# Edge MLP of a graph network: the second layer's bias copied into the message's PSUM bank by ScalarE, in place of a product with rows of ones

## The chip, the cores and the metric

The kernel runs on one core of a Trainium2 chip. The metric is the device time of one execution in microseconds. A core has TensorE (matmuls, results into PSUM, a memory of eight banks of 128 partitions x 512 float32), VectorE and ScalarE (elementwise work, both read and write SBUF and PSUM), GpSimd (here it issues gathers and scatters) and SyncE (issues plain DMAs). Each engine works through its own instructions in order, and semaphores order them between engines.

## The reference

Four graph layers run over the same 625 nodes of 512 features and 10625 edges. Each gets the normed, rectified rows `h` of `x`, and its result is added to `x`. The change lies in the third one, whose edge part is:

```
src, dst = (edge_index[0], edge_index[1])
edge_feat = jnp.concatenate([x[src], x[dst], edge_attr], axis=-1)
h = mish(edge_feat @ W1 + b1)
messages = mish(h @ W2 + b2)
agg = jax.ops.segment_sum(messages, dst, num_segments=x.shape[0])
```

with `mish(x) = x * tanh(softplus(x))`, 64 edge attributes, and `b2` a row of 512 values drawn with a spread of 0.1. The node part behind it and the fourth layer are untouched.

## The kernel before, in words

The products of the node features with W1 are made ahead for all nodes and stored as two tables in HBM. The edges are sorted by destination group into NS = 87 blocks of 128 edges. The stage of interest walks over these blocks; between this stage and its neighbours stands a barrier of all engines.

**Per block t**, in the order of the data:

- GpSimd gathers the row of table i for each edge and adds that of table j by a second gather (`gather_i` L1007, `add_j` L1015), nine blocks in flight.
- TensorE, `pre(t)` (L1156): four transposes of that sum into one bank (L1164), then four products of the edge attributes with their part of W1 on top (L1167, eight passes), so that the bank holds the hidden layer before its mish, turned.
- mish is worked out from e = exp(z) as z * (1 - 2 / (e * (e + 2) + 2)). ScalarE makes the exponential out of the bank (`grow_exp(0, t)`, L1119). VectorE clamps it (L1063) and makes e * (e + 2) (`top`, L1065). ScalarE takes the logarithm (`log_of`, L1124) and the exponential of its negative (`invert`, L1129), which is the reciprocal. VectorE multiplies with the bank (`finish_hidden`, L1072, semaphore mish0); the factor -2 sits in W2, scaled once at L1100.
- TensorE: the bias product (`bias(t)`, L1175), 64 rows of ones by 64 rows of which three hold b2 split into three bf16 parts and the others zero, into the same bank, which it starts anew. Then `message(t)` (L1184), eight passes of hidden x W2 on top of it.
- The same chain of ScalarE and VectorE with layer index 1 gives the message (`finish_message`, L1087, semaphore mish1). ScalarE rounds it (`high_part`, L1135), VectorE takes the remainder (`split_message`, L1094, semaphore mes_lo).
- VectorE makes a 128x128 table of which edge goes to which node (`one_hot`, L1080); TensorE adds both parts of the message over the edges by two products with it (`seg_sum`, L1199) into one of five banks.

Banks 5, 6 and 7 turn round; `pre(t)` and `message(t)` use the same one for every t of 1 and more, so that `pre(t + 3)` waits for mish1 of block t.

**The order** is written by hand, one turn s after the other, on each engine:

```
TensorE:  message(s-1); pre(s+1), with bias(s) inside it; seg_sum(s-2)
ScalarE:  exp of message s-1; exp of hidden s+1; log and invert of message s-1;
          log and invert of hidden s+1; high_part(s-1)
VectorE:  clamp and top of message s-1; one_hot(s-1); clamp and top of hidden s+1;
          finish_message(s-1); finish_hidden(s+1); split_message(s-1)
```

`bias(s)` stands behind the first attribute product of `pre(s+1)` and waits for mish0 of block s. The last block's bias stands ahead of its own message.

**Ahead of the first turn** TensorE turns the attributes of all blocks (88 transposes, L1208), ScalarE copies them out (L1139), VectorE makes the ones, the zeros and the three parts of b2 (L1048 to L1057), and SyncE loads b2 (2 KB, L986), the attribute weights (L987) and W2 (L988), and puts the three parts of b2 into place with three DMAs (L992).

Of the kernel before, what the change touches and what calls it, by code (L numbers as in the profile page):

```python
# [8 lines left out]
F32 = mybir.dt.float32  # L9
F32R = mybir.dt.float32r  # L10
BF16 = mybir.dt.bfloat16
FP16 = mybir.dt.float16
I32 = mybir.dt.int32
ALU = mybir.AluOpType
# [3 lines left out]
P = 128  # L18
N = 625
E = 10625  # L20
D = 512
# [23 lines left out]
def gnn_stack(nc, a, out):  # L45
    ctx = ExitStack()
    with ctx:
        def sb(name, shape, dt, where=ctx):
            return where.enter_context(nc.sbuf_tensor(name, shape, dt))
# [909 lines left out]
        with p3:  # L959
# [1 line left out]
            attr = sb("attr", [ED, SC * P], F32, p3)  # L961
            w_attr = sb("w_attr", [ED, D], F32, p3)
            w2 = sb("w2", [P, KT, D], F32, p3)
            b2_in = sb("b2_in", [1, D], F32, p3)
            b2_rows = sb("b2_rows", [P, D], BF16, p3)[ED:P, :]
            ones = sb("ones", [P, P], BF16, p3)[ED:P, :]
            pair_sum = sb("pair_sum", [P, GOT3, D], F32, p3)
            grow = [sb(f"grow{l}", [P, 2, D], F32, p3) for l in range(2)]
            hidT = sb("hidT", [P, 2, D], F32, p3)
# [2 lines left out]
            mes_lo = sb("mes_lo", [P, 2, D], F32R, p3)  # L972
            is_dst3 = sb("is_dst3", [P, HOT3, P], F32R, p3)
            none = mes[:, 0, :].bitcast(BF16)[:, 0:D]
            b2_flat = mes[0:1, :, :].rearrange("p b o -> p (b o)").bitcast(BF16)
            b2_part = [b2_flat[:, (j + 1) * D:(j + 2) * D] for j in range(3)]
            idx = rec[:, :, 0:2].bitcast(I32)
            pre_bank = lambda t: 5 + max(2 * t - 1, 0) % 3
            mes_bank = lambda t: 5 + (2 * t + 2) % 3
            N_TURN = SC // TURN_GROUP  # L980

# [1 line left out]

            @block.sync
            def _(sp):
                sp.dma_start(b2_in[:], a["b2_row"]).then_inc(sem("b2_in"), 16)  # L986
                sp.dma_start(w_attr[:], a["L2_gnn_W1"][2 * D:2 * D + ED, :]).then_inc(sem("w_attr_in"), 16)  # L987
                sp.dma_start(w2[:], a["L2_gnn_W2"].rearrange("(k p) o -> p k o", p=P)).then_inc(sem("w2_in"), 16)  # L988
                sp.wait_ge(sem("b2_split"), 6)
                sp.wait_ge(sem("b2_zero"), 1)  # L990
                for j in range(3):
                    sp.dma_start(b2_rows[j:j + 1, :], b2_part[j]).then_inc(sem("b2_rows"), 16)  # L992
                sp.wait_ge(sem("mes_mm"), 2)
                sp.dma_start(w3[:], a["L2_gnn_W3"].rearrange("(k p) o -> p k o", p=P)).then_inc(sem("w3_in"), 16)
                sp.dma_start(w4[:], a["L2_gnn_W4"].rearrange("(k p) o -> p k o", p=P)).then_inc(sem("w4_in"), 16)
                sp.dma_start(rows_in2[:], a["in_rows_in2"].broadcast_to((P, 4 * D)).rearrange("p (r o) -> p r o", r=4)).then_inc(sem("rows2_in"), 16)
                sp.dma_start(b3_col[:], a["in_b3_col"]).then_inc(sem("b3_in"), 16)
# [47 lines left out]
            @block.vector  # L1045
            def _(dve):

                nc.vector.memset(b2_rows, 0.0).then_inc(sem("b2_zero"), 1)  # L1048
                nc.vector.memset(ones, 1.0).then_inc(sem("b2_ones"), 1)
                nc.vector.memset(none, 0.0).then_inc(sem("none"), 1)  # L1050
                dve.wait_ge(sem("b2_in"), 16)
                for j in range(3):
                    if j:
                        dve.wait_ge(sem("b2_split"), 2 * j)
                    nc.vector.tensor_copy(b2_part[j], b2_in[:]).then_inc(sem("b2_split"), 1)
                    dve.wait_ge(sem("b2_split"), 2 * j + 1)
                    nc.vector.tensor_tensor(b2_in[:], b2_in[:], b2_part[j], ALU.subtract).then_inc(sem("b2_split"), 1)  # L1057

                def grown(l, t):

                    u = grow[l][:, t % 2, :]
                    dve.wait_ge(sem(f"exp{l}"), t + 1)
                    nc.vector.tensor_scalar(u, u, CLAMP, None, ALU.min).then_inc(sem(f"clamp{l}"), 1)  # L1063
                    dve.wait_ge(sem(f"clamp{l}"), t + 1)
                    nc.vector.scalar_tensor_tensor(u, u, 2.0, u, ALU.add, ALU.mult).then_inc(sem(f"top{l}"), 1)  # L1065

                def finish_hidden(t):

                    dve.wait_ge(sem("inv0"), t + 1)
                    if t >= 2:  # L1070
                        dve.wait_ge(sem("mes_mm"), t - 1)
                    nc.vector.scalar_tensor_tensor(hidT[:, t % 2, :], grow[0][:, t % 2, :], -0.5, PS[:, pre_bank(t), :],  # L1072
                                                   ALU.add, ALU.mult).then_inc(sem("mish0"), 1)

                def one_hot(t):
                    if t == 0:
                        dve.wait_ge(sem("rec_in"), 16)
                    if t >= HOT3:
                        dve.wait_ge(sem("sum_mm3"), t - HOT3 + 1)
                    nc.vector.tensor_scalar(is_dst3[:, t % HOT3, :], slot_of_col[:], rec[:, t, 2:3], None,  # L1080
                                            ALU.is_equal).then_inc(sem("is_dst3"), 1)

                def finish_message(t):
                    dve.wait_ge(sem("inv1"), t + 1)
                    if t >= 2:
                        dve.wait_ge(sem("mes_lo"), t - 1)
                    nc.vector.scalar_tensor_tensor(mes[:, t % 2, :], grow[1][:, t % 2, :], -0.5, PS[:, mes_bank(t), :],  # L1087
                                                   ALU.add, ALU.mult).then_inc(sem("mish1"), 1)

                def split_message(t):  # L1090
                    dve.wait_ge(sem("mes_hi"), t + 1)
                    if t >= 2:
                        dve.wait_ge(sem("sum_mm3"), t - 1)
                    nc.vector.tensor_tensor(mes_lo[:, t % 2, :], mes[:, t % 2, :], mes_hi[:, t % 2, :].bitcast(F32),  # L1094
                                            ALU.subtract).then_inc(sem("mes_lo"), 1)

                for s in range(-1, NS + 1):
                    if s == -1:
                        dve.wait_ge(sem("w2_in"), 16)
                        nc.vector.tensor_scalar(w2[:], w2[:], -2.0, None, ALU.mult).then_inc(sem("w2_scaled"), 1)  # L1100
                    if 0 <= s - 1 < NS:
                        grown(1, s - 1)
                        one_hot(s - 1)
                    if 0 <= s + 1 < NS:
                        grown(0, s + 1)
                    if 0 <= s - 1 < NS:
                        finish_message(s - 1)
                    if 0 <= s + 1 < NS:
                        finish_hidden(s + 1)
                    if 0 <= s - 1 < NS:  # L1110
                        split_message(s - 1)

            @block.scalar
            def _(act):
# [16 lines left out]
                def high_part(t):  # L1131
# [2 lines left out]
                        act.wait_ge(sem("sum_mm3"), t - 1)  # L1134
                    nc.scalar.copy(mes_hi[:, t % 2, :], mes[:, t % 2, :]).then_inc(sem("mes_hi"), 1)  # L1135

                for j in range(N_TURN):
                    act.wait_ge(sem("attr_tp"), j + 1)
                    nc.scalar.copy(attr[:, j * D:(j + 1) * D], PS[0:ED, j % 8, :]).then_inc(sem("attr_T"), 1)  # L1139
                for s in range(-1, NS + 1):  # L1140
                    if 0 <= s - 1 < NS:
                        grow_exp(1, s - 1, mes_bank(s - 1))
# [7 lines left out]
                        invert(0, s + 1)  # L1150
                    if 0 <= s - 1 < NS:
                        high_part(s - 1)

            @block.tensor
            def _(pe):
                def pre(t):  # L1156

                    pe.wait_ge(sem(f"pair3_{t % GOT3}"), 16 * (t // GOT3) + 16)
                    if t == 2:
                        pe.wait_ge(sem("mish0"), 1)  # L1160
                    if t >= 3:
                        pe.wait_ge(sem("mish1"), t - 2)
                    for k in range(KT):
# [2 lines left out]
                    for k in range(KT):  # L1166
                        m = nc.tensor.matmul(PS[:, pre_bank(t), k * P:(k + 1) * P], w_attr[:, k * P:(k + 1) * P],  # L1167
                                             attr[:, t * P:(t + 1) * P], start=False, stop=True, skip_group_check=True)
                        if k == 0 and t:
                            bias(t - 1)  # L1170
                    m.then_inc(sem("pre_mm"), 1)

                def bias(t):
                    pe.wait_ge(sem("mish0"), t + 1)
                    nc.tensor.matmul(PS[:, mes_bank(t), :], ones, b2_rows, start=True, stop=False, skip_group_check=True)  # L1175

                def message(t):

                    chunk = None
                    if t == NS - 1:  # L1180
                        bias(t)
                    o = PS[:, mes_bank(t), :]
                    for k in range(KT):
                        m = nc.tensor.matmul(o, hidT[:, t % 2, k * P:(k + 1) * P], w2[:, k, :], start=False,  # L1184
# [29 lines left out]
                    nc.tensor.matmul(PS[:, c, :], none[:, 0:P], none, start=True, stop=False, skip_group_check=True)  # L1214
                pe.wait_ge(sem("w_attr_in"), 16)
                for s in range(-1, NS + 2):
                    if s == 0:
                        pe.wait_ge(sem("b2_ones"), 1)
                        pe.wait_ge(sem("b2_rows"), 48)
                    if s == 1:  # L1220
                        pe.wait_ge(sem("w2_scaled"), 1)
                    if 0 <= s - 1 < NS:
# [437 lines left out]
```

## Time and profile before

| | |
|---|---|
| median of three runs | 1295.84 us (1293.26 to 1300.98) |
| profiled execution, its own time | 1297.59 us |
| its span | 1295.8 us |
| granted TensorE clock, mean of the span | 0.973 |
| stage of the edge MLP in the trace | 535 to 1052 us |
| steady part of it | about 563 to 1040 us |
| steps | 87 |

The span goes from the first to the last instruction of the profiled execution; its own time has what lies around it as well. Times in the rows are microseconds, mean durations ns. A record's duration has the filling and draining of the engine in it, so the start of the next instruction can lie before the end of the one before. The granted clock is given as a share of the full 2.4 GHz.

### The profile page before, as it was taken

How to read it: one execution, taken by the hardware profiler on the slowest of the kernel's cores; microseconds unless marked ns; L12 is line 12 of the kernel's file. 1: busy time of each engine (PE TensorE's matmuls, PEld its weight loads, DVE VectorE, ACT ScalarE, POOL GpSimd, SP SyncE). 2: the span in 40 equal slices, each digit the busy share in tenths (PEclk: the TensorE clock that was granted, in tenths of full speed). 3: DMA queues.
4: the chain of work that ended last, by engine and by line, in shares of the span. 5: the costliest groups of instructions: out<-in, count | busy, mean ns of one | idle time of the engine just before them, and what ended most of it. 6: DMA issues, size and time to landing. Idle time of an engine off the chain costs nothing. (4 is left out here: it accounts for less than half of the span.)

```text
span 1295.8 us, 15266 instructions
## 1 busy us (share of the span) xinstructions
PE 1214.3 (94%) x4908; PEld 646.6 (50%) x4908; DVE 795.6 (61%) x1576; ACT 556.7 (43%) x975; POOL 510.5 (39%) x442
## 2 busy tenths in 40 slices
PE   7898899599999999899999999999999979899995
PEld 3433433244544444555555555555555546445552
DVE  5764564667322323267778777777778756846663
ACT  1021211210110211357777777777777733225552
POOL 1111111253242000277766666666666100047661
PEclk9999899799999999889999999999999989999998
DMA  8699686555400201496544444444444020036662
GB/s 342 230 342 362 236 316 247 180 185 166 175 15 8 95 1 43 117 221 154 109 94 94 95 97 92 96 91 98 92 96 82 1 68 1 17 123 201 185 183 79
DMA packets 59444, 175.86 MB, mean 136 GB/s; under 512 B 12485, under 2 KB 13029, under 8 KB 52584
## 3 DMA queue, kind: packets, MB, share of 16 engines
q0 software_dynamic: 32496, 76.65, 25.0%
q1 hardware_dynamic: 26872, 98.23, 20.9%
q8 instruction: 43, 0.70, 0.2%
q14 instruction: 33, 0.27, 0.1%
HBM read 160.32 MB, written 14.52 MB: 135 GB/s over the span
## 5 line engine op out<-in xcount | busy, mean ns | idle before, releaser
L1184 PE MATMUL PS<-w,hidT 128*128 128x512 f32 x696 | 315.1, 595 | 0.0
L542 POOL DMA_INDIRECT rec_scratch<-rec_src,slot_row x84 | 99.4, 1184 | 287.6 <-DMA rec_scratch<-rec_src,slot_row 234.1
L1184 PEld LDWEIGHTS PS<-w,hidT 128*128 128x128 f32 x696 | 132.3, 191 | 134.0 <-issue 126.7
L1007 POOL DMA_INDIRECT pair_sum<-table_i,counts_rec x87 | 87.4, 1004 | 219.1 <-POOLq L63 130.7
L1015 POOL DMA_INDIRECT pair_sum<-table_j,counts_rec x87 | 147.6, 1697 | 30.7 <-issue 26.2
L1119 ACT ACTIVATE grow<-PS 128x512 f32<-128x512 f32 x174 | 104.0, 598 | 119.1 <-PE PS L1167 83.9
L1280 POOL DMA_INDIRECT u_space<-table_j,rec x87 | 82.3, 946 | 130.8 <-DMA table_j<-agg_rows 94.1
L269 PE MATMUL PS<-is_src,is_dst 128*128 128x512 bf16 x420 | 111.6, 397 | 20.4 <-DVE is_src L575 19.3
L1124 ACT ACTIVATE grow<-grow,two 128x512 f32<-128x512 f32 x174 | 124.8, 717 | 5.0 <-DVE grow L1065 4.9
L1065 DVE SCALAR_TENSOR_TENSOR grow<-grow 128x512 f32<-128x512 f32 x174 | 120.6, 693 | 6.0
L317 PE MATMUL PS<-w_rel,hT 128*128 128x512 f32 x240 | 107.6, 605 | 13.6 <-DMA w_rel<-w_scratch 11.9
L1129 ACT ACTIVATE grow<-grow 128x512 f32<-128x512 f32 x174 | 109.6, 630 | 5.5
L1167 PE MATMUL PS<-attr,w_attr 64*128 64x128 f32 x696 | 101.5, 286 | 0.0
L1024 POOL DMA_INDIRECT rec_scratch<-rec_src,slot_row x84 | 86.4, 1028 | 38.3 <-issue 23.2
L1063 DVE TENSOR_SCALAR grow<-grow 128x512 f32<-128x512 f32 x174 | 74.4, 428 | 40.0 <-ACT grow L1119 31.0
L1072 DVE SCALAR_TENSOR_TENSOR hidT<-grow,PS 128x512 f32<-128x512 f32 x87 | 59.8, 687 | 58.1 <-ACT grow L1129 58.1
L850 ACT COPY stage<-PS 128x512 f32<-128x512 f32 x48 | 28.1, 586 | 154.6 <-PE PS L299 154.6
L1167 PEld LDWEIGHTS PS<-attr,w_attr 64*128 64x128 f32 x696 | 84.5, 188 | 14.5 <-issue 14.5
L1362 DVE TENSOR_TENSOR pair<-PS,u_space 128x512 f32<-128x512 f32 x87 | 60.2, 692 | 47.5 <-issue 39.7
L1540 PE MATMUL PS<-relu,is_src 128*128 128x512 f32 x174 | 88.5, 592 | 0.0
L269 PEld LDWEIGHTS PS<-is_src,is_dst 128*128 128x128 bf16 x420 | 37.6, 101 | 93.9 <-DVE is_src L575 39.4
L1467 ACT ACTIVATE relu<-pair 128x512 f32<-128x512 f32 x87 | 54.9, 631 | 60.3 <-DVE pair L1362 60.3
(216 smaller groups left out, 1795.2 us busy)
## 6 DMA issues: line engine op xcount, KB each, us to landing
ring<-basis_rows SPq DMA_DIRECT2D x48, 1024.0 KB, 7.4
ring<-basis_low SPq DMA_DIRECT2D x30, 512.0 KB, 4.6
w_scratch<-stage SPq DMA_DIRECT2D x96, 32.0 KB
rec_scratch<-ring POOLq DMA_DIRECT2D x2, 1496.0 KB, 14.8
counts_rec<-rec_scratch SPq DMA_DIRECT2D x1, 2992.0 KB, 10.7
rec_scratch<-rec_src,slot_row POOLq DMA_INDIRECT x168, 3.5
root<-L_gnn_root SPq DMA_DIRECT2D x2, 1024.0 KB, 7.8
w_rel<-w_scratch SPq DMA_DIRECT2D x1, 2048.0 KB
```

The source lines that it names most:

```text
L269: nc.tensor.matmul(PS[:, c, :], is_dst[:, t % HOT, c * P:(c + 1) * P], is_src[:, t % HOT, 0:512], start=first, stop=last, skip_group_check ...
L317: m = nc.tensor.matmul(PS[:, bank, :], hT[:, k, c * P:(c + 1) * P], w[:, k, :], start=(k == 0), stop=(k == KT - 1))
L542: nc.gpsimd.indirect_dma_start(out=rec3_dram, out_offset=bass.IndirectOffsetOnAxis(ap=slot_row[:, 1, t:t + 1], axis=0), in_=rec, in_offset ...
L1007: nc.gpsimd.indirect_dma_start(out=pair_sum[:, t % GOT3, :], out_offset=None, in_=tables[0][0], in_offset=bass.IndirectOffsetOnAxis(ap=idx ...
L1015: nc.gpsimd.indirect_dma_start(out=pair_sum[:, t % GOT3, :], out_offset=None, in_=tables[0][1], in_offset=bass.IndirectOffsetOnAxis(ap=idx ...
L1065: nc.vector.scalar_tensor_tensor(u, u, 2.0, u, ALU.add, ALU.mult).then_inc(sem(f"top{l}"), 1)
L1119: nc.scalar.activation(grow[l][:, t % 2, :], PS[:, bank, :], ACT.Exp).then_inc(sem(f"exp{l}"), 1)
L1124: nc.scalar.activation(u, u, ACT.Ln, bias=two[:]).then_inc(sem(f"ln{l}"), 1)
L1129: nc.scalar.activation(u, u, ACT.Exp, scale=-1.0).then_inc(sem(f"inv{l}"), 1)
L1167: m = nc.tensor.matmul(PS[:, pre_bank(t), k * P:(k + 1) * P], w_attr[:, k * P:(k + 1) * P], attr[:, t * P:(t + 1) * P], start=False, stop= ...
L1184: m = nc.tensor.matmul(o, hidT[:, t % 2, k * P:(k + 1) * P], w2[:, k, :], start=False, stop=(k == KT - 1), skip_group_check=True)
L1540: nc.tensor.matmul(PS[:, bass.ds(chunk, 1), :].rearrange("p c o -> p (c o)"), is_src5[:, t % HOT5, :], relu5[:, t % PAIR5, :], start=False ...
```

## The change

ScalarE writes b2, which now lies in SBUF on all 128 partitions, into the message's bank by a plain copy, `bias(t)`, behind the wait for mish0 of block t. It stands at the end of ScalarE's turn, behind `high_part`. `message(t)` on TensorE waits for that copy and adds onto what lies in the bank. The bias product, the ones, the three-part split of b2 and their DMAs go, and so do TensorE's waits for them and the wait of `pre(2)`. b2 is loaded by one broadcast DMA to 128 partitions, still the first on SyncE's queue, and ScalarE waits for it once ahead of its turns. Block 0 now goes through the same bank in `pre` and `message` (7 in place of 5 for `pre(0)`).

```diff
@@ tiles, banks
-            b2_in = sb("b2_in", [1, D], F32, p3)
-            b2_rows = sb("b2_rows", [P, D], BF16, p3)[ED:P, :]
-            ones = sb("ones", [P, P], BF16, p3)[ED:P, :]
+            b2_all = sb("b2_all", [P, D], F32, p3)
...
-            pre_bank = lambda t: 5 + max(2 * t - 1, 0) % 3
+            pre_bank = lambda t: 5 + (2 * t - 1) % 3
@@ sync
-                sp.dma_start(b2_in[:], a["b2_row"]).then_inc(sem("b2_in"), 16)
+                sp.dma_start(b2_all[:], a["b2_row"].broadcast_to((P, D))).then_inc(sem("b2_in"), 16)
...
-                sp.wait_ge(sem("b2_split"), 6)
-                sp.wait_ge(sem("b2_zero"), 1)
-                for j in range(3):
-                    sp.dma_start(b2_rows[j:j + 1, :], b2_part[j]).then_inc(sem("b2_rows"), 16)
@@ vector
-                nc.vector.memset(b2_rows, 0.0).then_inc(sem("b2_zero"), 1)
-                nc.vector.memset(ones, 1.0).then_inc(sem("b2_ones"), 1)
                 nc.vector.memset(none, 0.0).then_inc(sem("none"), 1)
-                dve.wait_ge(sem("b2_in"), 16)
-                for j in range(3):
-                    if j:
-                        dve.wait_ge(sem("b2_split"), 2 * j)
-                    nc.vector.tensor_copy(b2_part[j], b2_in[:]).then_inc(sem("b2_split"), 1)
-                    dve.wait_ge(sem("b2_split"), 2 * j + 1)
-                    nc.vector.tensor_tensor(b2_in[:], b2_in[:], b2_part[j], ALU.subtract).then_inc(sem("b2_split"), 1)
@@ scalar
+                def bias(t):
+                    act.wait_ge(sem("mish0"), t + 1)
+                    nc.scalar.copy(PS[:, mes_bank(t), :], b2_all[:]).then_inc(sem("bias"), 1)
+
                 for j in range(N_TURN):
...
+                act.wait_ge(sem("b2_in"), 16)
                 for s in range(-1, NS + 1):
...
                     if 0 <= s - 1 < NS:
                         high_part(s - 1)
+                    if 0 <= s + 1 < NS:
+                        bias(s + 1)
@@ tensor
                 def pre(t):
...
-                    if t == 2:
-                        pe.wait_ge(sem("mish0"), 1)
...
-                        if k == 0 and t:
-                            bias(t - 1)
...
-                def bias(t):
-                    pe.wait_ge(sem("mish0"), t + 1)
-                    nc.tensor.matmul(PS[:, mes_bank(t), :], ones, b2_rows, start=True, stop=False, skip_group_check=True)
-
                 def message(t):
...
-                    if t == NS - 1:
-                        bias(t)
+                    pe.wait_ge(sem("bias"), t + 1)
...
-                    if s == 0:
-                        pe.wait_ge(sem("b2_ones"), 1)
-                        pe.wait_ge(sem("b2_rows"), 48)
```

## Rows read from the trace of the kernel before

**Rows 1.** The page, busy time of each engine, share of the span, instructions

```profile
PE 1214.3 (94%) x4908; PEld 646.6 (50%) x4908; DVE 795.6 (61%) x1576; ACT 556.7 (43%) x975; POOL 510.5 (39%) x442
```

**Rows 2.** Busy time by stretch: PE, PEld, DVE, ACT, POOL, then PEclk, DMA share, GB/s

```profile
563.00:1040.00 477.00, 476.88 (x1954) 277.79 (x1951) 377.17 (x680) 360.90 (x596) 302.56 (x244) 1.00 0.47 98
```

**Rows 3.** Timeline of PE, one step: start, us, operation, [idle before <-releaser]

```profile
643.19 3.59 PE L1184 MATMUL PS<-w,hidT 128*128 128x512 f32 x8
646.62 0.60 PE L1164 MATMUL PS<-ident,pair_sum 128*128 128x128 f32 x4
...
647.16 0.39 PE L1175 MATMUL PS<-b_rows,ones 64*128 64x512 bf16 x1
647.36 0.94 PE L1167 MATMUL PS<-attr,w_attr 64*128 64x128 f32 x7
648.23 0.50 PE L1199 MATMUL PS<-mes_hi,is_dst 128*128 128x512 f32 x1
...
648.80 3.60 PE L1184 MATMUL PS<-w,hidT 128*128 128x512 f32 x8
```

**Rows 4.** Timeline of ACT in the same step

```profile
641.20 0.60 ACT L1119 ACTIVATE grow<-PS 128x512 f32<-128x512 f32 x1 [0.38 <-PE PS L1184]
642.73 0.60 ACT L1119 ACTIVATE grow<-PS 128x512 f32<-128x512 f32 x1 [0.93 <-PE PS L1167]
643.22 0.71 ACT L1124 ACTIVATE grow<-grow,two 128x512 f32<-128x512 f32 x1
...
644.54 0.72 ACT L1124 ACTIVATE grow<-grow,two 128x512 f32<-128x512 f32 x1
645.30 0.63 ACT L1129 ACTIVATE grow<-grow 128x512 f32<-128x512 f32 x1
645.83 0.60 ACT L1135 CAST mes_hi<-mes 128x512 fp32r<-128x512 f32 x1
```

**Rows 5.** Timeline of DVE in the same step

```profile
641.83 0.43 DVE L1063 TENSOR_SCALAR grow<-grow 128x512 f32<-128x512 f32 x1 [0.19 <-ACT grow L1119]
642.29 0.69 DVE L1065 SCALAR_TENSOR_TENSOR grow<-grow 128x512 f32<-128x512 f32 x1
642.90 0.32 DVE L1080 TENSOR_SCALAR is_dst<-slot_of_col,counts_rec 128x128 fp32r<-128x128 f32 x1
643.36 0.43 DVE L1063 TENSOR_SCALAR grow<-grow 128x512 f32<-128x512 f32 x1
643.82 0.69 DVE L1065 SCALAR_TENSOR_TENSOR grow<-grow 128x512 f32<-128x512 f32 x1
644.63 0.69 DVE L1087 SCALAR_TENSOR_TENSOR mes<-grow,PS 128x512 f32<-128x512 f32 x1
645.96 0.69 DVE L1072 SCALAR_TENSOR_TENSOR hidT<-grow,PS 128x512 f32<-128x512 f32 x1 [0.65 <-ACT grow L1129]
646.56 0.69 DVE L1094 TENSOR_TENSOR mes_lo<-mes,mes_hi 128x512 fp32r<-128x512 f32 x1
```

**Rows 6.** Timeline of ACT, the second message exponential and the last but one

```profile
567.68 0.60 ACT L1135 CAST mes_hi<-mes 128x512 fp32r<-128x512 f32 x1
568.20 0.60 ACT L1119 ACTIVATE grow<-PS 128x512 f32<-128x512 f32 x1
...
1039.91 0.60 ACT L1119 ACTIVATE grow<-PS 128x512 f32<-128x512 f32 x1 [0.39 <-PE PS L1184]
```

**Rows 7.** Timeline of all engines, first steps and last message product

```profile
555.05 0.69 DVE L1072 SCALAR_TENSOR_TENSOR hidT<-grow,PS 128x512 f32<-128x512 f32 x1 [1.45 <-ACT grow L1129]
...
557.37 5.64 PE L1184 MATMUL PS<-w,hidT 128*128 128x512 f32 x8
563.05 0.60 ACT L1119 ACTIVATE grow<-PS 128x512 f32<-128x512 f32 x1 [2.37 <-PE PS L1184]
...
1041.56 3.70 PE L1184 MATMUL PS<-w,hidT 128*128 128x512 f32 x8
```

**Rows 8.** DMA issues (KB each, us to landing), and the timeline's scaling of w2

```profile
table_i<-ring SPq DMA_DIRECT2D x5, 256.0 KB, 2.0
```

```profile
544.94 1.51 DVE L1100 TENSOR_SCALAR w<-w 128x2048 f32<-128x2048 f32 x1 [4.85 <-DMA w<-L_gnn_W]
```

More of the change, by code:

```diff
@@ L974, in gnn_stack @@
             none = mes[:, 0, :].bitcast(BF16)[:, 0:D]
-            b2_flat = mes[0:1, :, :].rearrange("p b o -> p (b o)").bitcast(BF16)
-            b2_part = [b2_flat[:, (j + 1) * D:(j + 2) * D] for j in range(3)]
             idx = rec[:, :, 0:2].bitcast(I32)
-            pre_bank = lambda t: 5 + max(2 * t - 1, 0) % 3
+            pre_bank = lambda t: 5 + (2 * t - 1) % 3
             mes_bank = lambda t: 5 + (2 * t + 2) % 3
```

## The prediction

> **What bounds the kernel now.** I read the page first. TensorE is busy for 94% of the span, the other engines for 61% and less [rows 1]. A share over the whole span mixes stages with different limits, and the change touches only the edge MLP, so the next view is the busy time of that stage alone. From 563 to 1040 us TensorE is busy for 476.9 of 477.0 us at a granted clock of 1.00 (its 2.4 GHz level), VectorE for 79% and ScalarE for 76% [rows 2]. The reader is to see that TensorE has no gap there, and that the two others have room only on average.
>
> The third view is the timeline of one step, engine by engine. On TensorE a message product starts at 643.19 and the next at 648.80, and every piece in between follows the one before without idle time [rows 3]. From the message exponential of 568.20 to that of 1039.91 [rows 6] there are 84 steps: 471.71 / 84 = 5.616 us each. ScalarE waits twice in a step: 0.38 us for the message product, then 0.93 us for the next block's hidden product [rows 4]. VectorE waits 0.19 us and 0.65 us, both times for ScalarE [rows 5]. So TensorE sets the step now, and the other two follow it with some slack. How much slack is the whole question, and it isn't the 24% of idle time that ScalarE shows. The copy comes at one fixed place in ScalarE's order, so it costs whatever the chain through that place leaves free.
>
> **Removed from TensorE.** The bias product starts at 647.16 and the next piece at 647.36 [rows 3], so it holds TensorE for 0.20 us of each step (its record of 0.39 us runs on beside the next). TensorE alone would then need 5.616 - 0.20 = 5.41 us, and 86 steps of this give 17 us. This gain is real only if nothing else needs more than 5.41 us.
>
> **Added to ScalarE.** 87 copies of 128x512, each behind the wait for `finish_hidden` of the same block (semaphore mish0), last in ScalarE's turn. Queued behind it is the exponential of the next message, and VectorE's whole turn begins with that one. Before, that exponential stood behind `high_part`, which doesn't wait for `finish_hidden`. So a ring closes which the old order left open. I add it up from start to start, from the step of ScalarE and VectorE that starts at 641.20 [rows 4, 5]:
>
> - message exponential 641.20 to its clamp 641.83: 0.63
> - clamp to its product `top1` 642.29: 0.46
> - to `one_hot` 642.90: 0.61. No wait here, it is VectorE's own order; the 0.69 us record overlaps the next by 0.08
> - `one_hot` to the hidden clamp: 0.24. The row shows 0.46, but there the clamp still waits for the hidden exponential, which ends at 643.33. In the new order that exponential starts right behind the message's and is ready in time. So the link is the record of 0.32 less the same overlap of 0.08; bounds 0.24 to 0.32
> - hidden clamp 643.36 to its product 643.82: 0.46
> - to the logarithm 644.54: 0.72
> - to the inversion 645.30: 0.76
> - to `finish_hidden` 645.96: 0.66
> - to the bias copy: 0.72, its record of 0.69 and the 0.03 that passes from VectorE to ScalarE at 644.54
> - bias copy to the next message exponential: 0.52, see below
>
> The sum is 5.78 us. The other branches are inside it. The message logarithm and inversion are done before the hidden logarithm can start (3.12 us into the turn by the first six links; the message branch needs 0.63 + 0.46 + 0.72 + 0.76 + 0.53 = 3.10). `high_part` runs beside `finish_hidden`, as now. The split starts 0.60 behind `finish_hidden` and ends 4.54 + 0.60 + 0.69 = 5.83 us into the turn, so the sum over edges that needs it can't begin before 0.05 us into the next, by my estimate at 0.1 to 0.3; TensorE waits there. From then it needs 0.57 (648.23 to 648.80) and 3.60 us until the message is done [rows 3], so by 4.5 us, 1.3 us before ScalarE comes to read it. `pre` is done another 4.84 - 3.60 + 0.1 us later, at 5.8, and ScalarE reads it at 5.78 + 0.50 = 6.28. TensorE is off the ring.
>
> **Price of the copy.** The trace of before has no ScalarE instruction that writes PSUM. The nearest row is `high_part`, also a plain 128x512 copy out of SBUF, with a message exponential right behind it: 567.68 to 568.20, 0.52 us [rows 6]. The low end is 0.49, the shortest from one full-width ScalarE start to the next (642.73 to 643.22 [rows 4]); the high end is 0.60, the whole record of `high_part` with no overlap at all. I take 0.52, because reading is the same and width decides most. The ring then is 5.75 to 5.86 us by this term, and up to 0.08 more by the `one_hot` link.
>
> The Trainium skill (Perfetto Trace Analysis, Optimizing Scalar/DVE Operations) gives ScalarE a fixed cost of about 93 ns per instruction on SBUF but 51 ns on PSUM. No row here shows a ScalarE write to PSUM; if that rule holds for it, the copy would take an estimated 0.48 us, the ring 5.74 us, and the sum below would be 9.4 us in place of 12.9.
>
> **The ends of the stage.** At the start TensorE stands still inside the second `pre` until `finish_hidden` of block 0 (555.05 + 0.69), runs the bias product, finishes `pre`, and starts the first message at 557.37 [rows 7]. With the copy, `pre` is done long before. The copy runs from 555.77 to 556.4 and the message starts then: -0.9 us. The first step, from 563.05 (5.68 us after 557.37) to 568.20, takes only 5.15 us now, since there is no sum over edges in it; in the ring it takes 5.78: +0.6 us. At the end the last message product starts at 1041.56 [rows 7], 1.65 us after the message exponential of 1039.91 [rows 6]; without the bias product and with the split done earlier relative to ScalarE it starts some 1.0 us after it: -0.6 us.
>
> **Loads and preparation.** Six VectorE instructions, two memsets and three small DMAs of the bias rows go. Nobody waits for them: they run while the attributes are turned, long before the first bias product. On SP's queue the bias DMA grows from 2 KB to a broadcast of 256 KB, ahead of w_attr and w2; no other queue is passed. A transfer of 256 KB lands in about 2.0 us [rows 8]. w2 is scaled at 544.94 [rows 8], 12 us before its first use, so this cover holds. The first gathers share the DMA engines with it; bounds 0 to 1 us, I take 0, since TensorE comes to them behind the turning of the attributes. The ScalarE wait for the bias is met long before by then. The removed wait in `pre` for block 2 had been met as well.
>
> **The sum.** 84 steps x (5.78 - 5.616) = +13.8; -0.9, +0.6, -0.6: +12.9 us. The profiled execution took 1297.59 us (span 1295.8), so its like would be 1310.5. The median of the runs shown, 1295.84, is 1.75 lower; on it the sum gives 1308.7. The links are read to 0.01 us, and ten of them rounded carry 84 times into the sum; I say 1308.
>
> **Rivals.**
>
> *A. TensorE decides alone: faster.* If the ring had the slack that the 76% of ScalarE suggests, TensorE's 5.41 us would be the step, and the time 1295.84 - 17 - 1 = 1278 us. The place is the same one, the copy ahead of the message exponential. The point from which it decides is a ring below 5.41 us, so 0.37 us less than my sum. For it speaks that TensorE has no idle time in [rows 2]; against it that each link is a measured dependence, and even a copy of zero length leaves 5.26 us, so 0.15 us for a copy whose neighbours take 0.49 and more. The Trainium skill (Perfetto Trace Analysis, Identifying Performance Opportunities) says that improving a kernel generally means improving its most contended engine; that rule would give this result. Chance 0.08.
>
> *B. The ring is there but no longer than the old step: no change.* Several links would have to be shorter by 0.12 us and more together, say a copy that frees ScalarE after 0.43 and a `one_hot` link under 0.2. The step is then 5.60 to 5.68 and the time 1294 to 1300 us. For it speaks that two of the ten links are inferred and not seen. Chance 0.13.
>
> *C. A dear copy.* Writing PSUM takes longer than writing SBUF or doesn't overlap with the PSUM read behind it. With 0.72 us, the longest ScalarE record of this width [rows 4], the ring is 5.98 us and the time 1325 us. TensorE's waits would grow to over 0.5 us in a step. Its clock stayed at 1.00 through the whole stage, but no stretch of that stage has such gaps, so that it would stay there is assumed. Chance 0.05.
>
> *Forecast.* A ring of 5.70 to 5.88 us, 1302 to 1317 us, likeliest 1308. Chance 0.74.
>
> **How the numbers follow.** About 0.5%, 6.5 us, is what a measurement of this kernel can tell from no change. Slower by more than that, above 1302.3: the forecast but for a small edge of it, 0.73, and C, 0.05: together 0.78. Within 0.5%: B and that edge: 0.14. Faster: A, 0.08. The range leaves out A and C and most of what lies beyond a copy without overlap; it takes in most of B: 1298 to 1317 us.
>
> **What would show it.** In the profile of the changed kernel: the message product's starts lie 5.7 to 5.9 us apart; TensorE has a gap of some 0.3 us in each step, ahead of the sum over edges, released by VectorE's mes_lo; ScalarE's message exponential no longer waits for TensorE but follows the copy by about 0.52 us; the copy starts 0.72 us after `finish_hidden`; the hidden clamp follows `one_hot` without idle time. I am wrong if the message exponential still shows idle time released by TensorE (then A, with a step of 5.41), or if the copy's record is far from 0.60 us (B or C).

## The result and the profile after

The changed kernel takes 1305.63 us (median of six runs, 1300.85 to 1309.23) against 1294.86 us for the kernel before beside it: a ratio of 1.0078, 95% interval 1.0045 to 1.011. It is slower by 10.8 us, and the interval reaches from 5.8 to 14.2 us. On the prediction's footing, 1295.84, that is 1306 us, where 1308 was said.

The page of the changed kernel, busy time of the engines, to be held against [rows 1]:

```profile
PE 1215.8 (93%) x4821; PEld 645.1 (49%) x4821; DVE 782.6 (60%) x1568; ACT 597.5 (46%) x1062; POOL 507.4 (39%) x442
```

TensorE has 87 instructions fewer, 4821 for 4908, and its busy time hasn't fallen. That should stop the reader: 87 products of 0.39 us by their records are gone. ScalarE has 87 more and is busy for 41 us more.

The steady stretch (columns as in [rows 2]):

```profile
563.00:1040.00 477.00, 469.96 (x1825) 271.17 (x1823) 359.08 (x662) 389.73 (x662) 294.61 (x245) 1.00 0.46 99
```

TensorE, busy for 476.9 us of this stretch before, now has 7.0 us of gaps, and ScalarE went from 76% to 82%. The clock is the same. An engine at 82% doesn't look like the bound, so the views of one step have to tell. The timeline of ScalarE:

```profile
644.50 1.08 ACT L1101 ACTIVATE grow<-PS 128x512 f32<-128x512 f32 x2
646.31 0.72 ACT L1106 ACTIVATE grow<-grow,two 128x512 f32<-128x512 f32 x1 [0.73 <-DVE grow L1047]
647.07 0.63 ACT L1111 ACTIVATE grow<-grow 128x512 f32<-128x512 f32 x1
647.60 0.71 ACT L1106 ACTIVATE grow<-grow,two 128x512 f32<-128x512 f32 x1
648.34 0.63 ACT L1111 ACTIVATE grow<-grow 128x512 f32<-128x512 f32 x1
648.88 0.60 ACT L1117 CAST mes_hi<-mes 128x512 fp32r<-128x512 f32 x1
649.72 0.59 ACT L1121 COPY PS<-b_all 128x512 f32<-128x512 f32 x1 [0.25 <-DVE hidT L1054]
650.25 1.08 ACT L1101 ACTIVATE grow<-PS 128x512 f32<-128x512 f32 x2
```

The two exponentials at 644.50 and 650.25 no longer wait for TensorE (0.38 and 0.93 us of idle time in [rows 4]); they follow the bias copy and each other so closely that the view merges them. All idle time of ScalarE is now released by VectorE. VectorE in the same step, to be held against [rows 5]:

```profile
645.12 0.43 DVE L1045 TENSOR_SCALAR grow<-grow 128x512 f32<-128x512 f32 x1 [0.58 <-ACT grow L1101]
645.59 0.69 DVE L1047 SCALAR_TENSOR_TENSOR grow<-grow 128x512 f32<-128x512 f32 x1
646.20 0.28 DVE L1062 TENSOR_SCALAR is_dst<-slot_of_col,counts_rec 128x128 fp32r<-128x128 f32 x1
646.39 0.42 DVE L1045 TENSOR_SCALAR grow<-grow 128x512 f32<-128x512 f32 x1
646.85 0.69 DVE L1047 SCALAR_TENSOR_TENSOR grow<-grow 128x512 f32<-128x512 f32 x1
...
649.00 0.69 DVE L1054 SCALAR_TENSOR_TENSOR hidT<-grow,PS 128x512 f32<-128x512 f32 x1 [0.59 <-PE PS L1164]
649.61 0.69 DVE L1076 TENSOR_TENSOR mes_lo<-mes,mes_hi 128x512 fp32r<-128x512 f32 x1
```

The first clamp waits 0.58 us for ScalarE's exponential (0.19 before). The row at 649.00 names TensorE as the releaser. It starts at 648.34 + 0.63 + 0.03, the end of ScalarE's inversion and the usual 0.03 us, and a message product ended at nearly the same moment. In most steps the view names ScalarE, and in every step `finish_hidden` starts 0.03 us after the inversion's end.

From start to start the ring is: message exponential 644.50, clamp 645.12 (0.62), top 645.59 (0.47), message logarithm 646.31 (0.72), its inversion 647.07 (0.76), hidden logarithm 647.60 (0.53), its inversion 648.34 (0.74), `finish_hidden` 649.00 (0.66), bias copy 649.72 (0.72), next message exponential 650.25 (0.53). The sum is 5.75 us, and it is the step.

TensorE, to be held against [rows 3]:

```profile
643.05 0.60 PE L1151 MATMUL PS<-ident,pair_sum 128*128 128x128 f32 x4
643.58 1.16 PE L1154 MATMUL PS<-attr,w_attr 64*128 64x128 f32 x8
644.83 0.49 PE L1179 MATMUL PS<-mes_hi,is_dst 128*128 128x512 f32 x1
...
645.39 3.59 PE L1164 MATMUL PS<-w,hidT 128*128 128x512 f32 x8
```

From the first attribute pass to the sum over edges it takes 1.25 us here. Before it took 647.15 to 648.23, 1.08 us, with the bias product in between. So the removal of the product shortened nothing, and a gap of 0.17 us was added. The message product is done at 645.39 + 3.59 = 648.98; ScalarE reads it at 650.25, 1.3 us later.

The first steps and the last, all engines, to be held against [rows 6, 7]:

```profile
557.80 5.37 PE L1164 MATMUL PS<-w,hidT 128*128 128x512 f32 x8 [3.03 <-ACT PS L1121]
563.21 0.60 ACT L1101 ACTIVATE grow<-PS 128x512 f32<-128x512 f32 x1 [1.07 <-PE PS L1164]
569.21 1.27 ACT L1101 ACTIVATE grow<-PS 128x512 f32<-128x512 f32 x2
...
1053.39 0.59 ACT L1101 ACTIVATE grow<-PS 128x512 f32<-128x512 f32 x1
1057.87 0.60 ACT L1101 ACTIVATE grow<-PS 128x512 f32<-128x512 f32 x1
```

Between the second message exponential and the last but one lie 84 steps: (1053.39 - 569.21) / 84 = 5.764 us, against 5.616.

### The profile page after: what moved, and what is told of

Its sections match the earlier page's. It is cut to its first block and busy times, and to the rows that moved or that the text cites. A ratio compares the mean times of both kernels' runs of the same rounds, so it can differ in the third digit from the quotient of the medians.

```text
span 1307.4 us, 15167 instructions
## 1 busy us (share of the span) xinstructions
PE 1215.8 (93%) x4821; PEld 645.1 (49%) x4821; DVE 782.6 (60%) x1568; ACT 597.5 (46%) x1062; POOL 507.4 (39%) x442
## 5 line engine op out<-in xcount | busy, mean ns | idle before, releaser
L542 POOL DMA_INDIRECT rec_scratch<-rec_src,slot_row x84 | 105.9, 1261 | 287.5 <-DMA rec_scratch<-rec_src,slot_row 231.7
L1007 POOL DMA_INDIRECT pair_sum<-table_j,counts_rec x87 | 139.4, 1603 | 31.2 <-issue 26.2
L1016 POOL DMA_INDIRECT rec_scratch<-rec_src,slot_row x84 | 85.1, 1014 | 36.0 <-issue 22.9
L1101 ACT ACTIVATE grow<-PS 128x512 f32<-128x512 f32 x174 | 94.4, 591 | 5.0 <-PE PS L1154 3.9
```

Source lines behind the costliest of these rows:

```text
L542: nc.gpsimd.indirect_dma_start(out=rec3_dram, out_offset=bass.IndirectOffsetOnAxis(ap=slot_row[:, 1, t:t + 1], axis=0), in_=rec, in_offset ...
L1007: nc.gpsimd.indirect_dma_start(out=pair_sum[:, t % GOT3, :], out_offset=None, in_=tables[0][1], in_offset=bass.IndirectOffsetOnAxis(ap=idx ...
L1101: nc.scalar.activation(grow[l][:, t % 2, :], PS[:, bank, :], ACT.Exp).then_inc(sem(f"exp{l}"), 1)
```

## The experiments

Two theories to begin with. The **ring**: the copy costs because its wait for `finish_hidden` stands ahead of the next message exponential. Against it: ScalarE has too much to do wherever the copy stands, or writing PSUM or TensorE's new wait makes the loss. The table gives for each kernel the typical step, and the time from the first `high_part` to the last, 86 steps with the uneven ones at both ends. Ratios are to the kernel before, run beside each on the same chip. The expectations in microseconds stand on the 1295.84 us of the prediction; beside these runs the kernel before took 1309.26, 1314.68 or 1313.46 us, so steps and ratios are what is compared.

| kernel | step, us | first to last high_part, us | ratio (95%) |
|---|---|---|---|
| before | 5.62 | 481.6 | 1 |
| changed | 5.75 | 494.1 | 1.0078 (1.0045 to 1.011) |
| gap | 5.61 | 481.1 | 0.9987 (0.9964 to 1.0011) |
| no_bias | 5.61 | 480.9 | 0.9975 (0.9947 to 1.0004) |
| spare_wait | 5.75 | 494.4 | 1.0071 (1.0047 to 1.0096) |
| spare_free | 5.61 | 481.6 | 0.998 (0.9955 to 1.0004) |
| half_copy | 5.62 | 481.0 | 0.9976 (0.9947 to 1.0004) |
| one_hot_later | 5.75 | 493.9 | 1.0086 (1.0055 to 1.0118) |
| rows_shared | 5.83 | 499.3 | 1.0159 (1.0123 to 1.0195) |
| gap_padded | 5.23 | 448.7 | 0.9713 (0.9686 to 0.974) |
| end_padded | 5.75 | 493.5 | 1.0092 (1.0057 to 1.0127) |
| product_padded | 5.44 | 466.6 | 0.9931 (0.991 to 0.9953) |

### gap: the copy at another place

```diff
                         grow_exp(1, s - 1, mes_bank(s - 1))
+                    if 0 <= s < NS:
+                        bias(s)
                     if 0 <= s + 1 < NS:
                         grow_exp(0, s + 1, pre_bank(s + 1))
...
-                    if 0 <= s + 1 < NS:
-                        bias(s + 1)
```

Expected: 

> The copy of bias(s) moved from the end of ScalarE's turn to between the message exponential and the hidden exponential of the next turn, where ScalarE waited 0.93 us in the kernel before. Ring theory (the copy costs because its wait for finish_hidden stands ahead of the message exponential): the ring opens, TensorE decides, step 5.616 - 0.20 = 5.41 us, message exponential again released by TensorE, time about 17 us below the kernel before, 1275 to 1280. Rival (ScalarE is simply too full, or writing PSUM gets in the way of others, wherever the copy stands): the step stays at 5.7 to 5.75 us and the time at 1303 to 1308.

Measured: step 5.61 us, ratio 0.9987. The timeline of ScalarE:

```profile
700.48 0.60 ACT L1101 ACTIVATE grow<-PS 128x512 f32<-128x512 f32 x1 [0.39 <-PE PS L1164]
700.98 0.59 ACT L1121 COPY PS<-b_all 128x512 f32<-128x512 f32 x1
702.00 0.60 ACT L1101 ACTIVATE grow<-PS 128x512 f32<-128x512 f32 x1 [0.43 <-PE PS L1154]
```

Half of this went as the ring theory said. The loss is gone, the exponential is again released by TensorE, and the copy took 0.50 of the 0.93 us for which ScalarE waited there. The same copy into the same bank costs nothing at this place, so the rival is out. But neither theory had said 5.61 us: the step was to fall to 5.41 without the bias product on TensorE, and it is that of the kernel before.

### no_bias: neither product nor copy

```diff
-                    if 0 <= s + 1 < NS:
-                        bias(s + 1)
...
-                    pe.wait_ge(sem("bias"), t + 1)
+                    pe.wait_ge(sem("mish0"), t + 1)
...
-                        ... w2[:, k, :], start=False,
+                        ... w2[:, k, :], start=(k == 0),
```

Expected: 

> The changed kernel without the copy: the bias of the second layer is left out, the first pass of the message product starts the bank, and TensorE waits for finish_hidden itself. It measures what taking the bias product off TensorE is worth by itself. Ring theory: step 5.41 us (0.20 less than 5.616), about 1278 us. Rival (the bias product was hidden in the loading of weights and cost TensorE little): step 5.5 to 5.6 us, 1288 to 1295.

Measured: 5.61 us, below even the rival's gain of nearly nothing. The timeline of TensorE:

```profile
703.07 1.16 PE L1152 MATMUL PS<-attr,w_attr 64*128 64x128 f32 x8
704.16 0.50 PE L1177 MATMUL PS<-mes_hi,is_dst 128*128 128x512 f32 x1
```

The eight attribute passes alone hold TensorE for 1.09 us; in the kernel before, eight passes and the bias product held it for 1.08 (647.15 to 648.23). The product's price was nothing. Ahead of the product of [rows 3] stands one attribute pass, which that group leaves out:

```profile
647.15 0.37 PE L1167 MATMUL PS<-attr,w_attr 64*128 64x128 f32 x1
```

The pass and the product start 0.01 us apart, and the next pass 0.21 us behind the first. In no_bias the second pass starts 0.21 us behind the first too (703.07 and 703.28), though nothing stands between them; the later ones follow at 0.11.

### spare_wait and spare_free: a copy added to the kernel before, with and without the wait

```diff
+                def spare_copy(t):
+                    act.wait_ge(sem("mish0"), t + 1)
+                    nc.scalar.copy(spare[:, 1, :], spare[:, 0, :]).then_inc(sem("spared"), 1)
...
                         high_part(s - 1)
+                    if 0 <= s + 1 < NS:
+                        spare_copy(s + 1)
```

spare_free is the same without the line that waits. Expected of spare_wait: 

> The kernel before, bias product and all, with one more 128x512 copy from SBUF to a spare SBUF tile at the end of ScalarE's turn, behind the wait for finish_hidden of the same block, read by nobody. Ring theory: the ring closes as in the changed kernel, step 5.75 to 5.77 us, about 1295 + 12 = 1307 us, though TensorE has lost nothing of its work and waits for no copy. Rival (TensorE's wait for the copy, or the write to PSUM, makes the loss): step 5.62 us, time as before.

Expected of spare_free: 

> The same spare copy at the same place, but without the wait for finish_hidden. Ring theory: the turn of ScalarE is 3.10 + 0.74 + 0.53 + 0.51 + 0.53 = 5.41 us with it, under TensorE's 5.616, so the step and the time are those of the kernel before, within 0.3%. Rival (what costs is ScalarE's time in all, not the wait): the same loss as with the wait, 1305 to 1308 us.

Measured: 1.0071 with the wait, 0.998 without. The timelines of ScalarE, first with, then without:

```profile
701.91 0.62 ACT L1141 COPY spare<-spare 128x512 f32<-128x512 f32 x1 [0.25 <-DVE hidT L1074]
702.43 1.08 ACT L1121 ACTIVATE grow<-PS 128x512 f32<-128x512 f32 x2
```

```profile
704.93 0.61 ACT L1140 COPY spare<-spare 128x512 f32<-128x512 f32 x1
705.46 0.58 ACT L1121 ACTIVATE grow<-PS 128x512 f32<-128x512 f32 x1
```

Without the wait the copy fills the 0.38 us that ScalarE waited for the message: from `high_part` to the message exponential it is 1.03 us (704.43 to 705.46) in place of 0.99 in the kernel before (645.83 to 646.82). The 0.04 us over are taken up by ScalarE's wait for the hidden product, now 0.88 to 0.90 us long in place of 0.93. With it, a copy that nobody reads, in a kernel that keeps its product and whose TensorE waits for no copy, makes the whole loss: 494.4 us against the changed kernel's 494.1. The loss is made by a copy behind that wait at that place in the order.

### half_copy and one_hot_later: what the ring is made of

```diff
-                    nc.scalar.copy(PS[:, mes_bank(t), :], b2_all[:]).then_inc(sem("bias"), 1)
+                    nc.scalar.copy(PS[:, mes_bank(t), 0:D // 2], b2_all[:, 0:D // 2]).then_inc(sem("bias"), 1)
```

Expected: 

> The changed kernel with the copy cut to 256 of 512 columns; the bias is left out of the other half, which keeps the hidden layer under the message. Ring theory: 256 columns less are 0.21 us, the ring falls from 5.75 to 5.54 us, below TensorE's 5.61, so the step is 5.61 and the time within 0.3% of the kernel before. Rival (a fixed loss by the wait itself, not by the copy's length): step 5.75 us as in the changed kernel.

Measured: 5.62 us, ratio 0.9976. The timeline of ScalarE:

```profile
705.56 0.38 ACT L1121 COPY PS<-b_all 128x256 f32<-128x256 f32 x1 [0.25 <-DVE hidT L1054]
705.87 0.59 ACT L1101 ACTIVATE grow<-PS 128x512 f32<-128x512 f32 x1
```

From start to start the copy takes 0.31 in place of 0.53 us, 0.22 less, more than the 0.14 by which the ring exceeded TensorE's step. The wait is still there, 0.25 us long, and does no harm: it costs only as much as the ring is longer than TensorE's step.

```diff
                         grown(1, s - 1)
-                        one_hot(s - 1)
...
                         grown(0, s + 1)
                     if 0 <= s - 1 < NS:
+                        one_hot(s - 1)
                         finish_message(s - 1)
```

Expected: 

> The changed kernel with one_hot moved behind clamp and top of the hidden block on VectorE. By the prediction's own ring, which runs through one_hot, the step would fall by its link of 0.20 us to 5.55 us and TensorE's 5.61 would decide. By the profile of the changed kernel the message's logarithm and inversion, in ScalarE's order, take 3.10 us to the hidden logarithm and are the longer branch by about 0.03 us: then the step stays at 5.75 us.

Measured: 5.75 us, as in the changed kernel. The timelines of VectorE and of ScalarE in one step:

```profile
705.30 0.69 DVE L1047 SCALAR_TENSOR_TENSOR grow<-grow 128x512 f32<-128x512 f32 x1
705.91 0.31 DVE L1062 TENSOR_SCALAR is_dst<-slot_of_col,counts_rec 128x128 fp32r<-128x128 f32 x1
```

```profile
704.96 0.72 ACT L1106 ACTIVATE grow<-grow,two 128x512 f32<-128x512 f32 x1 [0.73 <-DVE grow L1047]
705.72 0.63 ACT L1111 ACTIVATE grow<-grow 128x512 f32<-128x512 f32 x1
706.25 0.71 ACT L1106 ACTIVATE grow<-grow,two 128x512 f32<-128x512 f32 x1
```

VectorE's product for the hidden block now ends at 705.99, and still the hidden logarithm starts at 706.25, when ScalarE is through with the message's inversion. So the ring runs through ScalarE's order (logarithm, inversion, logarithm), not through `one_hot`.

### rows_shared: why the product was free

The kernel before has ones and bias rows on partitions 64 to 127, and the attributes on 0 to 63.

```diff
-            b2_rows = sb("b2_rows", [P, D], BF16, p3)[ED:P, :]
-            ones = sb("ones", [P, P], BF16, p3)[ED:P, :]
+            b2_rows = sb("b2_rows", [P, D], BF16, p3)[0:ED, :]
+            ones = sb("ones", [P, P], BF16, p3)[0:ED, :]
```

Expected: 

> The kernel before with ones and the bias rows on partitions 0 to 63, those of the attribute product, in place of 64 to 127; nothing else changes. Theory from the runs without the product (step 5.61 still): the bias product runs beside the attribute passes because it uses the other half of TensorE's rows, and costs nothing. On the same half it has to take its turn: 512 columns, 0.21 us, step 5.82 us, about 18 us above the kernel before. Rival (it was free for another reason, for instance because weight loads set the pace of these passes): step 5.62 us, time as before.

Measured: 5.83 us, ratio 1.0159. The timeline of TensorE:

```profile
700.40 0.48 PE L1167 MATMUL PS<-attr,w_attr 64*128 64x128 f32 x2
700.72 0.38 PE L1175 MATMUL PS<-b_rows,ones 64*128 64x512 bf16 x1
700.94 0.83 PE L1167 MATMUL PS<-attr,w_attr 64*128 64x128 f32 x6
701.69 0.50 PE L1199 MATMUL PS<-mes_hi,is_dst 128*128 128x512 f32 x1
```

The block takes 1.29 us in place of 1.08: moved to the rows that the attributes use, the same product costs 0.21 us. On the other half of the rows it ran beside them. The Trainium skill (TensorEngine Tiling (Array Packing), Key Properties) says that different tiles of the array can load weights and multiply in parallel; the two starts 0.01 us apart agree.

That it cost nothing at all has a second reason. The product needs 0.21 us by itself, and one attribute pass 0.11. The missing 0.10 us are the pause behind the first pass, which no_bias has as well. spare_wait shows the product away from that pause: there it waits for a `finish_hidden` that ends at 701.88, and starts beside the third pass.

```profile
701.93 0.39 PE L1184 MATMUL PS<-b_rows,ones 64*128 64x512 bf16 x1
701.93 0.93 PE L1176 MATMUL PS<-attr,w_attr 64*128 64x128 f32 x6
702.79 0.50 PE L1208 MATMUL PS<-mes_hi,is_dst 128*128 128x512 f32 x1
```

Its last six passes take 0.86 us (701.93 to 702.79) with the product beside them, against 0.75 behind it in rows_shared (700.94 to 701.69). So on the other rows, but without the pause, the product costs 0.11 us, half of its price on the same rows. The time of spare_wait doesn't show this, since TensorE doesn't decide there.

### gap_padded, end_padded, product_padded: one width for all products

In no_bias the eight 64-row passes took 1.09 us, though in the middle of them both passes and weight loads are only 0.11 us apart. The same section of the Trainium skill (TensorEngine Tiling (Array Packing), Key Properties) says that changing the tiling mode drains TensorE. In gap_padded the attribute product has 128 rows:

```diff
-            attr = sb("attr", [ED, SC * P], F32, p3)
-            w_attr = sb("w_attr", [ED, D], F32, p3)
+            attr = sb("attr", [P, SC * P], F32, p3)
+            w_attr = sb("w_attr", [P, D], F32, p3)
...
+                nc.vector.memset(w_attr[ED:P, :], 0.0).then_inc(sem("pad"), 1)
+                nc.vector.memset(attr[ED:P, :], 0.0).then_inc(sem("pad"), 1)
```

Expected: 

> The gap kernel (copy between the two exponentials), with the attribute product widened from 64 to 128 partitions, the upper 64 rows of both operands zero, so that TensorE never changes between products of 128 and of 64 rows. In the profile of the run without bias the next weight load stands about 0.2 us late both ahead of and behind the 64-row passes. Change-of-rows theory: two such pauses of 0.1 to 0.2 us go, step 5.61 down to 5.3 to 5.4 us, 17 to 26 us below the kernel before. Rival (the pauses belong to the float32 passes or to a change of operand, not to the number of rows): step 5.61 us, time as before.

Measured: 5.23 us, ratio 0.9713. The timeline of TensorE:

```profile
704.29 0.60 PE L1153 MATMUL PS<-ident,pair_sum 128*128 128x128 f32 x4
704.73 1.06 PE L1156 MATMUL PS<-attr,w_attr 128*128 128x128 f32 x8
705.54 0.48 PE L1181 MATMUL PS<-mes_hi,is_dst 128*128 128x512 f32 x1
```

From the transposes to the attribute passes it is 0.44 us (0.53 before, [rows 3] from 646.62 to 647.15), and the passes take 0.81 (1.09 in no_bias). Two pauses were expected to go, and three went: 0.09 us ahead of the first pass, 0.10 behind it and 0.17 behind the last (from its start to the sum over edges 0.20 us in no_bias, 0.03 here). Passes in the middle follow at 0.11 us with 64 and with 128 rows, so what costs is the change and not the 64 rows. Over 87 steps 0.37 us are 32 us; from the first `high_part` to the last it is 32.4 us less than in gap and 32.9 less than before. This version beats both kernels.

end_padded is the changed kernel with the same padding. Expected: 

> The changed kernel, copy at the end of ScalarE's turn, with the attribute product padded to 128 partitions as in gap_padded, which gave TensorE a step of 5.23 us. Ring theory: TensorE isn't on the ring, so the step stays at 5.75 us and the time about 12 us above the kernel before, though TensorE could go 0.5 us a step faster; its gaps grow to some 0.5 us. Rival (TensorE's own work still decides part of the step): the step falls by some of the 0.38 us, 5.4 to 5.6 us, faster than the kernel before.

Measured: 5.75 us, ratio 1.0092. The timeline of TensorE:

```profile
706.18 0.49 PE L1181 MATMUL PS<-mes_hi,is_dst 128*128 128x512 f32 x1 [0.27 <-DVE mes_lo L1078]
```

TensorE could go 0.5 us a step faster and gives all of it back; part of the gap now shows as a wait for mes_lo. With the copy at the end of the turn the 0.38 us that the padding takes off TensorE's step don't reach the time.

product_padded keeps the bias product and puts both products on 128 rows. Expected: 

> The kernel before, bias by a product, with both the attribute product and the bias product on all 128 partitions, rows without data being zero. Nothing can run beside anything, and the number of rows never changes. Theory: TensorE's step is the 5.23 us of gap_padded plus one pass of 512 bf16 columns, 0.21 to 0.22 us, so 5.45 us, about 14 us below the kernel before and 19 us above gap_padded: in a kernel of one width the copy in the gap is worth the product's columns. Rival (the product hides there too, or the copy is worth nothing anywhere): 5.23 us, the time of gap_padded.

Measured: 5.44 us, ratio 0.9931. The timeline of TensorE:

```profile
701.10 1.27 PE L1169 MATMUL PS<-attr,w_attr 128*128 128x128 f32 x8
702.12 0.48 PE L1201 MATMUL PS<-mes_hi,is_dst 128*128 128x512 f32 x1
```

The block takes 1.02 us against 0.81 in gap_padded. Once nothing can run beside the attribute passes the product costs its 0.21 us, and replacing it by a copy in the gap is worth 17.9 us from the first `high_part` to the last (466.6 against 448.7).

## Why the prediction was right, and the step that failed

**What bounds, and how it ends.** A ring over ScalarE and VectorE was to close through the copy's wait and take over from TensorE. It did, and spare_wait shows that it makes the whole of the loss. The message exponential lost its wait for TensorE, the copy starts 0.72 us after `finish_hidden` (649.00 to 649.72), and the message is ready 1.3 us before it is read, all as said.

**The links.** The sum was 5.78, the measured step is 5.75 in a typical turn and 5.764 on average. Eight of the ten links came within 0.02 us. The `one_hot` link, inferred as 0.24, is 0.19 (646.20 to 646.39). It had no weight, since the other branch, put at 3.10 us and dismissed as 0.02 us shorter, is the one that decides: 644.50 to 647.60 is 3.10. The copy's price, 0.52, is 0.53. The estimate of 0.48 us by the smaller fixed cost for PSUM in the Trainium skill (Perfetto Trace Analysis, Optimizing Scalar/DVE Operations) isn't borne out: into PSUM the next instruction starts 0.53 us after the copy, into SBUF (spare_wait) 0.52; only the record is shorter, 0.59 against 0.62.

**The step that failed** is "Removed from TensorE": the bias product holds TensorE for 0.20 us of each step, and without it TensorE needs 5.41. Taking it away gained nothing (no_bias: 5.61; gap: 5.61). I read 647.16 to 647.36 as the product's share of a queue, but the attribute pass at 647.15 and the product at 647.16 start 0.01 us apart: two products side by side. And the 0.20 us up to the next pass stay without the product (703.07 to 703.28 in no_bias). The forecast stood because TensorE isn't on the ring, so its length didn't enter the 84 steps. Three things built on it fell: rival A's 1278 us could not have come about (with an open ring the result is no change, as gap shows), the gap on TensorE is 0.14 us in the median step (none to 0.34, counted beyond the 0.20 us that no_bias has from the last attribute pass to the sum over edges) and not 0.3, and for the same reason the view mostly doesn't show its release by mes_lo. The release is there all the same: mes_lo ends at 650.30 (649.61 + 0.69) and the sum over edges starts at 650.55, 0.30 us into the turn, at the upper end of the estimate.

**The terms.** 84 steps: 84 x (5.764 - 5.616) = +12.4, for +13.8. The start, counted from the stage's first load (536.61 after, 535.02 before): the first message product starts 21.19 us after it against 22.35, -1.2 for -0.9, and the first message exponential 26.60 against 28.03, -1.4 in all. The forecast link itself was -0.9: from the end of `finish_hidden` of block 0 to that product it is 0.76 us (557.04 to 557.80) against 1.63 (555.74 to 557.37). The other -0.6 were not forecast: `finish_hidden` came 0.3 us earlier, behind a turning of the attributes of 12.06 and not 12.57 us, and the first message product took 5.37 and not 5.64 us. TensorE's granted clock was 0.50 from 557.40 to 560 before and 0.65 from 557.80 to 560 after. The first step took 6.00 us against 5.15, +0.85 for +0.6. The end, 1053.39 to 1057.87 against 5.39 us before: -0.9 for -0.6. Together +11.0 us for +12.9. From its first load to the next stage's first product the stage took 529.5 us in the profiled execution (536.61 to 1066.13) against 518.5 (535.02 to 1053.55), which is these 11.0; the medians lie 10.8 apart. So the forecast was 1.9 us too high, 1.4 of them because the ring was summed about 0.016 us too long. One remark on the range: with its start at 1298 it holds the upper third of B's 1294 to 1300 us, not most of it.

**Loads.** The broadcast cost nothing that can be seen: W2 is scaled at 546.16, 11.6 us before its first use. The second block's gather was 0.31 us late for TensorE, while TensorE had nothing urgent.

## What to carry to other kernels

When an instruction with a wait is added to an engine that isn't the bound, don't price it by the engine's idle share. Follow the order of that engine from the new wait round to itself, through every engine that answers it, and compare that ring with the bound's step; then look for a place in the same order where the engine waits anyway (here moving the copy behind one exponential took back the whole loss). Before crediting the removal of a small product, check whether it ran on rows of the array that its neighbours leave free, and whether the time up to the next start would stay without it.

## What the runs showed of the hardware that was not expected

A bf16 product of 64 x 512 cost TensorE nothing beside the first of the float32 passes on the other 64 rows (5.61 us with and without), 0.11 us beside the third (spare_wait), and 0.21 us on the same rows (5.83) or with every product on 128 rows (5.44 against 5.23). Going from products of 128 rows to products of 64 and back cost 0.09 + 0.10 + 0.17 us each time. Doubling the rows of the attribute product with zeros was therefore faster by 0.37 us a step, and, with the copy in the gap, the kernel by 2.9%. By the drain that the Trainium skill (TensorEngine Tiling (Array Packing), Key Properties) gives for a change of tiling mode such pauses are to be expected; the runs show only that they go with the change of rows, and not what the engine does in them.
